# Two chained cross-attentions: x and weights also passed in transposed, row-bias sums on VectorE, the orders of the steps anew

## The reference

```python
# layer 0: softmax over the QUERY axis, residual, layernorm
q = x @ Wq0 + bq0;  k = ctx @ Wk0 + bk0;  v = ctx @ Wv0 + bv0
w = softmax(q @ k.T / 16, axis=queries)
x = layernorm(w @ v + x) * gamma + beta
# layer 1: softmax over the context axis, residual
Q = x @ Wq1 + bq1;  K = ctx @ Wk1 + bk1;  V = ctx @ Wv1 + bv1
out = x + softmax(Q @ K.T / 16, axis=ctx) @ V @ Wo1 + bo1
```

## Time and profile before

| | us |
|---|---|
| timed runs, median of 3 | 467.65 (466.14 to 468.08) |
| profiled execution, first to last instruction (span) | 464.6 |
| TensorE busy | 443.7 (96%) |
| ScalarE busy | 383.7 (83%) |
| VectorE busy | 366.8 (79%) |
| GpSimd busy | 365.0 (79%) |
| granted TensorE clock | 1.000 |

### The profile page before, as it was taken

The page is one execution under the profiler, slowest core; times in us unless marked ns, Lnnn a source line. Parts: engine busy times, 40 slices in busy tenths (PEclk is TensorE's granted clock), DMA queues, the critical chain, the costliest instruction groups (busy, mean ns, idle before and its releaser), DMA issues.

```text
span 464.6 us, 7967 instructions
## 1 busy us (share of the span) xinstructions
PE 443.7 (96%) x2433; PEld 371.6 (80%) x2433; DVE 366.8 (79%) x898; ACT 383.7 (83%) x819; POOL 365.0 (79%) x321
## 2 busy tenths in 40 slices
PE   8798899999999999999999999999999999799796
PEld 8686667887888888888888878888888878687596
DVE  3798978788886988778787888779877887578774
ACT  4899889987999789987899879987899879872473
POOL 0567699979999799887999789987999699963400
PEclk9999999999999999999999999999999999999999
DMA  9400200021100210020200210001100010000001
GB/s 262 130 24 24 71 24 2 23 72 34 36 23 1 72 47 23 24 55 18 70 23 1 71 49 23 24 18 55 46 1 0 3 46 1 0 0 25 23 1 45
DMA packets 23896, 17.29 MB, mean 37 GB/s; under 512 B 1055, under 2 KB 23854, under 8 KB 23854
## 3 DMA queue, kind: packets, MB, share of 16 engines
q1 hardware_dynamic: 23706, 16.66, 11.8%
q10 hardware_dynamic: 148, 0.13, 0.1%
HBM read 12.59 MB, written 4.19 MB: 36 GB/s over the span
## 4 chain that ended last, share of the span: by engine, by line
PE 79%; ACT 8%; DVE 5%; POOL 4%; issue 4%; DVEq 0%; POOLq 0%; ACTq 0%
PE ps_l L654 11%; PE ps_l L655 10%; PE ps_l L656 9%; PE ps_s L800 9%; PE ps_s L654 8%; PE ps_s L656 8%; PE ps_s L655 8%; ACT p L1048 3%; PE ps_s L774 3%; PE ps_s L841 3%; DVE max L1257 2%; POOL wsum L1376 2%; PE ps_l L687 2%; ACT p L1001 2%; PE ps_s L768 2%
## 5 line engine op out<-in xcount | busy, mean ns | idle before, releaser
L1376 POOL TENSOR_TENSOR wsum<-wsum,p 128x512 f32<-128x512 f32 (+1 forms) x88 | 116.3, 1322 | 13.4 <-ACT p L1007 11.8
L1383 POOL TENSOR_TENSOR p_lo<-p,p_hi 128x512 fp32r<-128x512 f32 (+1 forms) x91 | 117.2, 1295 | 2.6 <-ACT p_hi L1015 2.4
L1001 ACT ACTIVATE p<-s_sb,min 128x512 f32<-128x512 f32 (+1 forms) x104 | 75.4, 726 | 7.5 <-DVE min L1171 5.3
L1171 DVE CUSTOM_DVE_ANT_0 s_sb<-ps_l,cb 128x512 f32<-128x512 f32 (+1 forms) x104 | 70.4, 685 | 13.3 <-ACT p L1001 5.5
L1007 ACT ACTIVATE p<-p,r 128x512 f32<-128x512 f32 (+1 forms) x104 | 74.9, 728 | 1.4 <-DVE r L1178 1.3
L1192 DVE TENSOR_TENSOR p1T_lo<-ps_s,p1T_hi 128x512 fp32r<-128x512 f32 (+1 forms) x91 | 60.6, 683 | 14.4 <-ACT p1T_hi L1056 13.9
L1257 DVE TENSOR_REDUCE max<-ps_s 128x1 f32<-128x804 f32 x58 | 57.1, 992 | 10.0 <-PE ps_s L656 8.6
L1056 ACT CAST p1T_hi<-ps_s 128x512 fp32r<-128x512 f32 (+1 forms) x91 | 52.0, 586 | 14.9 <-PE ps_s L800 12.1
L1015 ACT CAST p_hi<-p 128x512 fp32r<-128x512 f32 (+1 forms) x104 | 63.5, 624 | 0.5 <-PE ps_l L656 0.4
L1048 ACT ACTIVATE p<-ps_s,bias 128x1206 f32<-128x1206 f32 (+1 forms) x58 | 53.6, 927 | 3.6 <-DVE bias L1268 3.1
L800 PE MATMUL ps_s<-ident,p 128*128 128x128 f32 (+1 forms) x364 | 49.6, 273 | 1.5 <-ACT p L1048 1.5
(11 more groups left out here) (181 smaller groups left out, 1100.1 us busy)
## 6 DMA issues: line engine op xcount, KB each, us to landing
ctx_sb<-in_ctx_dram SPq DMA_DIRECT2D x24, 256.0 KB, 2.9
x_sb<-in_x_dram SPq DMA_DIRECT2D x8, 512.0 KB, 3.6
out_dram<-y_res SPq DMA_DIRECT2D x16, 256.0 KB, 2.2
p<-in_L_xattn_Wq_dram SPq DMA_DIRECT2D x2, 256.0 KB, 4.2
ctx_sb<-in_ctx_dram SPq DMA_DIRECT2D x8, 32.5 KB
...
```

The source lines that it names most:

```text
L1001: nc.scalar.activation(p0[0:m, ring0(i), :], s0_sb[0:m, (a + i) % 2, :], ACT.Exp, bias=min0[0:m, i:i + 1], scale=-1.0, accum_out=sum0[0:m, ...
L1171: nc.vector.tensor_tensor_reduce(out=s0_sb[0:m, (a + i) % 2, :], in0=ps_s0[0:m, (a + i) % 2, :], in1=cb[a % 2][0:m, :], scale=-SCALE, scal ...
L1376: nc.gpsimd.tensor_tensor(total, total, p0[0:m, ring0(i), :], ALU.add).then_inc(wsum_done, 1)
L1383: nc.gpsimd.tensor_tensor(p0_lo[0:m, h, :], p0[0:m, ring0(i), :], p0_hi[0:m, h, :].bitcast(F32), ALU.subtract).then_inc(p0_lo_done, 1)
```

## The change

The program gets six more inputs, transposed before the launch: x as [8, 256, 512], the two Wq, the two Wk and the second layer's Wv; the seven bias and scale vectors that are needed as columns come as one [128, 2, 7] array. x itself is still passed in.

- turn_x, x_turned, xT_low are gone; `load_xT` loads a batch's transposed x, and project_q0 takes two float32 matmuls.
- turn_wq, turn_wk, turn_vectors and turn_w1 are gone with their copies and the repeated columns; make_w0 and make_w1 work on the loaded transposes.
- weigh_u0 and sum_z0 become `row_bias0`, weigh_u1, bias_row1 and row_bias1 become a new `bias_row1`: for each, four multiply-and-sum instructions of 128 x 256 on VectorE, both inputs in SBUF.
- sum_rows0 transposes wsum by four transposes, and VectorE sums 512 columns in PSUM.
- All four orders are written anew, and the steady part begins at another place (a batch letter d, two ahead, is added). ctx_high waits for the scores of the batch that last used its buffer.

```diff
-                for c in range(EC):
-                    mm = split3(ps_misc[:], a0_hi[:, c, :], a0_lo[:, c, :], xT_hi[:, c, :], xT_lo[:, c, :],
-                                start=(c == 0), stop=(c == EC - 1))
+                for c in range(EC):
+                    mm = nc.tensor.matmul(ps_misc[:], a0_sb[:, c, :], xT_sb[a % 2][:, c, :], start=(c == 0), stop=(c == EC - 1))
...
-                    mm = nc.tensor.matmul(ps_misc[:, t:t + 1], wsum[a % 2][:, t * P:(t + 1) * P], ones[:, 0:1],
-                                          start=True, stop=True)
+                    mm = nc.tensor.transpose(ps_misc[:, t * P:(t + 1) * P], wsum[a % 2][:, t * P:(t + 1) * P], ident[:])
...
+            def load_xT(c):
+                if c >= 2:
+                    sp.wait_ge(qw0_ps, c - 1)
+                sp.dma_start(xT_sb[c % 2][:], xT[bass.ds(c, 1)].rearrange("o (c p) t -> p (o c) t", p=P)
+                             ).then_inc(xT_loaded[c % 2], 16)
...
             def pre0():
-                sp.dma_start(wq_sb[0], wq0.rearrange("(c p) h -> p c h", p=P)).then_inc(w_loaded[0], 16)
+                sp.dma_start(wqT[0], wqT0.rearrange("(h p) e -> p h e", p=P)).then_inc(w_loaded[0], 16)
+                load_xT(0)
                 load_x(0)
...
             for c in range(2, B + 3):
                 if c < B:
+                    load_xT(c)
                     for g in range(GROUPS):
                         load_ctx(c, g)
                     load_x(c)
...
+            def row_bias0(a, _):
+                if a == 0:
+                    dve.wait_ge(u0_done, 1)
+                if a >= 2:
+                    dve.wait_ge(c1_done, TB * (a - 1))
                 if a > 0:
                     dve.wait_ge(cb_ps, a)
+                dve.wait_ge(x_loaded[a % 2], 16 * (a // 2 + 1))
+                for t in range(TB):
+                    nc.vector.tensor_tensor_reduce(out=xr[:, t, :], in0=x_sb[a % 2][:, t, :], in1=u0_row[:], scale=1.0, scalar=0.0,
+                                                   op0=ALU.mult, op1=ALU.add, accum_out=z0[:, t:t + 1]).then_inc(z0_done, 1)
...
             def bias_row1(b, _):
-                dve.wait_ge(u1_part_done, b + 1)
-                nc.vector.tensor_reduce(c1_part[:], xr[:], AX_X, ALU.add).then_inc(c1_part_done, 1)
+                dve.wait_ge(xhat_done, TB * (b + 1))
+                if b == 0:
+                    dve.wait_ge(row1_made, MADE)
+                else:
+                    dve.wait_ge(bias1_done, TB * b)
+                for t in range(TB):
+                    nc.vector.tensor_tensor_reduce(out=xr[:, t, :], in0=xhat[:, t, :], in1=u1_gamma[:], scale=1.0,
+                                                   scalar=c1_const[:, 0:1], op0=ALU.mult, op1=ALU.add,
+                                                   accum_out=c1[:, t:t + 1]).then_inc(c1_done, 1)
...
             def bias_x0(a, _):
-                nc.vector.tensor_copy(rowsum0[:], ps_misc[:, 0:TB]).then_inc(rowsum_done, 1)
+                nc.vector.tensor_reduce(rowsum0[:], ps_misc[:].rearrange("p (t m) -> p t m", m=P), AX_X, ALU.add
+                                        ).then_inc(rowsum_done, 1)
```

More of the change, by code:

```diff
@@ new lines @@
+    ("p0_low", 1, 1), ("rsqrt_var", 0, 0), ("rsqrt_var", 0, 1), ("sum_weights", 1, 2), ("p0_low", 1, 2),
+    ("p0_low", 1, 3), ("sum_weights", 1, 3), ("ctx_low", 1, 1), ("sum_weights", 1, 4), ("sum_weights", 1, 5),
+    ("p0_low", 1, 4), ("p0_low", 1, 5), ("ctx_low", 1, 2), ("sum_weights", 1, 6), ("p0_low", 1, 6),
+    ("sum_weights", 1, 7), ("p0_low", 1, 7), ("p0_low", 1, 8), ("residual1", 0, 0), ("p0_low", 1, 9),
+    ("sum_weights", 1, 8), ("sum_weights", 1, 9), ("sum_weights", 1, 10), ("sum_weights", 1, 11),
@@ L309 @@
-    ("sum_weights", 6, 8), ("ctx_low", 6, 3), ("p0_low", 6, 9), ("sum_weights", 6, 9), ("p0_low", 6, 10),
-    ("residual1", 5, 0), ("p0_low", 6, 11), ("sum_weights", 6, 10), ("sum_weights", 6, 11), ("sum_weights", 6, 12),
-    ("p0_low", 6, 12), ("sum_weights", 7, 1), ("p0_low", 7, 0), ("ctx_low", 7, 0), ("rsqrt_var", 6, 0),
-    ("p0_low", 7, 1), ("p0_low", 7, 2), ("rsqrt_var", 6, 1), ("weigh_u1", 6, 0), ("ctx_low", 7, 1),
-    ("sum_weights", 7, 2), ("ctx_low", 7, 2), ("sum_weights", 7, 3), ("p0_low", 7, 3), ("p0_low", 7, 4),
@@ L314 @@
-    ("sum_weights", 7, 4), ("ctx_low", 7, 3), ("sum_weights", 7, 5), ("p0_low", 7, 5), ("p0_low", 7, 6),
-    ("sum_weights", 7, 6), ("sum_weights", 7, 7), ("sum_weights", 7, 8), ("p0_low", 7, 7), ("sum_weights", 7, 9),
-    ("p0_low", 7, 8), ("p0_low", 7, 9), ("sum_weights", 7, 10), ("p0_low", 7, 10), ("residual1", 6, 0),
-    ("sum_weights", 7, 11), ("p0_low", 7, 11), ("sum_weights", 7, 12), ("p0_low", 7, 12), ("rsqrt_var", 7, 0),
-    ("rsqrt_var", 7, 1), ("weigh_u1", 7, 0), ("residual1", 7, 0),
+    ("sum_weights", 6, 10), ("sum_weights", 6, 11), ("sum_weights", 6, 12), ("p0_low", 6, 11), ("p0_low", 6, 12),
@@ new lines @@
+    ("residual1", 5, 0), ("ctx_low", 7, 0), ("sum_weights", 7, 1), ("p0_low", 7, 0), ("rsqrt_var", 6, 0),
+    ("rsqrt_var", 6, 1), ("p0_low", 7, 1), ("p0_low", 7, 2), ("sum_weights", 7, 2), ("sum_weights", 7, 3),
+    ("p0_low", 7, 3), ("ctx_low", 7, 1), ("ctx_low", 7, 2), ("p0_low", 7, 4), ("sum_weights", 7, 4), ("p0_low", 7, 5),
+    ("sum_weights", 7, 5), ("sum_weights", 7, 6), ("p0_low", 7, 6), ("p0_low", 7, 7), ("sum_weights", 7, 7),
+    ("sum_weights", 7, 8), ("sum_weights", 7, 9), ("ctx_low", 7, 3), ("p0_low", 7, 8), ("p0_low", 7, 9),
@@ L319 @@
+    ("p0_low", 7, 10), ("sum_weights", 7, 10), ("sum_weights", 7, 11), ("sum_weights", 7, 12), ("p0_low", 7, 11),
+    ("p0_low", 7, 12), ("residual1", 6, 0), ("rsqrt_var", 7, 0), ("rsqrt_var", 7, 1), ("residual1", 7, 0),
 )
@@ L871, in make_a, with row_of @@
                 return mm
+            def row_of(ps, col, rows_in):
+                for h in range(EC):
+                    mm = nc.tensor.matmul(ps, col[:, h:h + 1].broadcast_to([P, P]), rows_in[:, h, :],
+                                          start=(h == 0), stop=(h == EC - 1))
+                return mm
             def keep_warm(n):
@@ L1114, in _ @@
+                act.dma_start(cols[:], columns).then_inc(cols_loaded, 16)
             steps = {f.__name__: f for f in (
-                x_turned, q0_high, bias0, ctx_high, ctx_split, exp0, norm0, p0_high, weighed0, y_turned, row_bias1, q1_high, exp1,
-                p1_turned, weighed1, p1_turned_half, weighed1_half, copy_w1)}
+                q0_high, bias0, ctx_high, ctx_split, exp0, norm0, p0_high, weighed0, y_turned, q1_high, exp1,
+                p1_turned, weighed1, p1_turned_half, weighed1_half, copy_w0, copy_w1)}
@@ L1350, in _ @@
             steps = {f.__name__: f for f in (
-                ctxT_low, xT_low, at0_low, bias_x0, q0_low, weigh_u0_first, sum_z0, max0, recip0, residual0, moments0, normalised, bias_row1,
+                ctxT_low, at0_low, bias_x0, q0_low, row_bias0, max0, recip0, residual0, moments0, normalised, bias_row1,
                 q1_low, rowmax1, bias1_of, recip1, p0_low_first, p1_low, p1_low_half, finish, prepare_w1)}
@@ L1429, in _ @@
             steps = {f.__name__: f for f in (
-                ctx_low, sum_weights, p0_low, rsqrt_var, weigh_u0, weigh_u1, residual1)}
+                ctx_low, sum_weights, p0_low, rsqrt_var, residual1)}
             pre0()
@@ L1447 @@
     for name in _INS:
-        a = np.ascontiguousarray(inputs[name])
+        if name == "columns":
+            a = np.stack([inputs[n] for n in COLUMNS]).reshape(len(COLUMNS), -1, P).transpose(2, 1, 0)
+        elif name in TURNED:
+            a = np.swapaxes(inputs[TURNED[name]], -1, -2)
+        else:
+            a = inputs[name]
+        a = np.ascontiguousarray(a)
         arrays[f"in_{name}_dram"] = a
```

360 lines of the change are left out of this document (112 added, 248 removed), and 467 rows, old and new, of tables (GPSIMD_HEAD, GPSIMD_STEADY, SCALAR_HEAD, SCALAR_STEADY).

## The result

The changed kernel takes 499.45 us (median of 4 runs, 498.41 to 500.01) against 467.38 (466.14 to 468.08): ratio 1.0691, 95% interval 1.0668 to 1.0713. I had forecast 458.5, range 451 to 474, with 0.19 on slower. The forecast is wrong by 41 us and in its sign.

The account below looks back on a forecast made before the run. TensorE was taken to bound the kernel, nearly always busy in the middle. Gains 6.7 + 1.9 + 1.0 + 2.0, less 2.5 for waiting passes, made 9.1 us: span 455.5, time 458.5 us, range 451 to 474.

Parts of the forecast that it names:

- TensorE, each batch: Net TensorE work removed, 0.91 us a batch; over seven batches plus batch 0's sums, a 6.7 us gain.
- The totals' 0.35: In sum_rows0, four transposes (0.44 us) replace column sums of wsum (0.79), 0.35 us less TensorE work.
- The two float32 matmuls, 1.72: In project_q0, the added pair of 512 columns takes 1.72 us, as the same pair does in project_q1.
- The start: Before batch 0's first max: it comes at 13.4 us instead of 15.35, a 1.9 us gain, bounds 0 and 3.
- the 1.0 for the second layer's weights: Dropping turn_w1's transposes on TensorE and two ScalarE copies gains 1.0 us, bounds 0.5 to 2.
- What the passes wait for: VectorE's eight new row-bias passes wait for GpSimd 0.1 us each: 0.35 a batch, 2.5 us lost in all.
- The 38.28 pass: A 0.793 us VectorE multiply-and-sum, read as starting its own time when a GpSimd pass ended at 38.78.
- rival 1: Row-bias group ahead of q1_low alternates with GpSimd's 6.4 us queue, 1.29 us a turn: 484.5 us, chance 0.2.
- The cover of 0.2 us: Slack ahead of q1_low: max0 ends at 4.5 us after normalised, TensorE wants its score buffer at 4.7.
- Other edits: Loads, ctx_high's new wait and residual1 priced at 0; bias_x0 meeting residual1's passes at 0 to 0.7 us each.
- GpSimd's relief (2.0): GpSimd losing two products gains 2.0 us of TensorE's idle time at the ends, bounds 0 and 6.
- the new order (at most 0.24 a batch): New order of steps: the middle holds 0.24 us of idle a batch to be won, no more.

Follow-up runs that it names:

- kernel 5: Kernel before the change with only the float32 projection from a loaded transposed x, without turn_x, x_turned, xT_low: 464.36 us, ratio 0.9941.
- kernel 11: Changed kernel with one-input row-bias sums, GpSimd waiting for normalised, and residual1 of batches 1 to 5 waiting for bias_x0: 468.98 us, ratio 1.0049.
- kernel 7: Kernel 6 with one wait more: GpSimd's first operation of the next batch waits for the end of bias_x0; 464.82 us, ratio 0.9958.
- kernel 6: Kernel 5 with the totals of the weights taken by four transposes and a 512-element VectorE reduction: 483.67 us, ratio 1.0359.
- kernel 1: Changed kernel with both row-bias groups as plain one-input sums, multiply by u and constant left out: 486.43 us, ratio 1.0411.
- kernel 12: Kernel before the change with only the row biases moved to VectorE's multiply-and-sum passes, in its old order: 518.19 us, ratio 1.1114.
- kernel 2: Changed kernel in its new orders with the row-bias products back on GpSimd and sums on VectorE: 504.32 us, ratio 1.0772.

## Why the prediction was wrong, by its steps

**TensorE, each batch (0.91).** Right in size where little waits: kernel 5 shows its 0.56, and kernel 11's periods hold 52.3 us of TensorE's work instead of 53.1. The changed kernel's page shows nothing of the 8 us that TensorE was to be less busy: 447.0 us against 443.7, and 52.88 a batch against 53.10. The clock at half adds up to 8.5, and a matmul's record behind a wait is longer (0.50 us at 239.12, 0.39 behind it); I did not break it down further. The totals' 0.35 did not show (0.04 in kernel 7); the step itself went from 0.81 to 0.36 us from its start to the next one's (202.90 in kernel 5, 208.66 in kernel 6), and what fills the difference I did not trace.

**The two float32 matmuls, 1.72.** Held with the clock full: the pair spans 1.88 us in the timeline, as project_q1's did before. In batch 1, in the stretch at half clock, it spans 3.26.

**The start (1.9).** First max at 14.03, so 1.3 us earlier than before and 0.6 later than said. Yet batch 0's normalised came at 60.03 against 56.77: 3.3 us lost. The rows of the start that show it, TensorE's, then VectorE's (in brackets idle time and cause):

```profile
25.76 0.50 PE L629 MATMUL ps_l<-p_hi,ctx_lo 128*128 128x512 f32 x1 [3.29 <-DVE p_lo L1076]
```

```profile
22.55 1.48 DVE L1203 TENSOR_TENSOR p<-p 128x256 f32<-128x256 f32 x1 [1.11 <-DMA p<-in_L_xattn_bo_dram]
23.95 1.75 DVE L1076 TENSOR_TENSOR p_lo<-p,p_hi 128x512 fp32r<-128x512 f32 x1
```

VectorE waits 1.11 us for a load, and then two passes meet GpSimd, which runs two sums of weights from 22.48 to 25.15. Behind the wait comes the first stretch at half clock, and the second lies around 60.03 itself.

I followed the start only up to the first max and took it for granted that what comes behind keeps its lead. Its 1.9 and the 3.3 make 5.2 of the 41 us, and the 1.0 for the second layer's weights is in no run by itself.

**What the passes wait for (2.5).** This is the step that failed. I had both ends, 0 and 1.29 us a pass, and chose 0.1 by 13 passes of p_lo that stand singly in batch 0, beside a half-full GpSimd. A single pass waits at most for the rest of one GpSimd pass; a group waits for one whole pass at each of its members, and the row for a group (0.42 from start to start) was taken where GpSimd stood still. The 38.28 pass was read too well: it ended 0.29 us behind the GpSimd pass (39.07 and 38.78), where a free one takes 0.48, so "to the hundredth" is wrong, though it did wait. And 0.1 for each of eight passes less 0.2 of cover makes 0.6 us a batch, not 0.35. The mechanism was rival 1, told with its 6.4 us queue. What was measured: 13.0 us for the two row-bias groups in this order (kernel 1), 51 in before's (kernel 12). The cover of 0.2 us that I worked out ahead of q1_low was near: bias_row1 ended 4.9 us after normalised instead of 3.3, and TensorE lost 1.22 of the difference of 1.6 there.

**Other edits.** "bias_x0 may now meet residual1's 0.74 us passes: 0 to 0.7 each" was in the text and not in the sum. Its passes took 0.96 instead of 0.48, three in a group. And as a group that would wait, normalised was not in the text at all. Both together are the greater part: from kernel 1 to kernel 11, 17.5 us, the clock's share in it included. I had asked which new instructions meet GpSimd; the question was which of all VectorE's groups meet it in the new order. With the totals I named the 0.69 us reduction as VectorE work (it is 0.67) and put it nowhere in time, although the four passes stand right behind it and GpSimd's next pass began 1.40 us after their start. Kernel 6 shows the price of that shift: 19 us.

**TensorE's clock.** The prediction had it at full speed throughout and no term for it. In the changed kernel it costs up to 8.5 us, and it goes with the long waits: what makes TensorE wait is paid a second time in part.

**GpSimd's relief (2.0), the new order (at most 0.24 a batch).** The bound on the order was one-sided: an order can win no more than the idle time, but it can lose whatever it moves together. GpSimd's relief is in no run by itself; in kernel 11 the stretch from the last normalised to the end is 41.3 us, before 40.1. And its products had also been a guard. weigh_u1 waited for xhat (0.85 us in the earlier trace rows) and weigh_u0 for VectorE's z (11.0 us in all in the earlier trace rows), so GpSimd stood still there. Kernel 2 shows the guard: with weigh_u1 back behind rsqrt_var, normalised fell from 0.850 to 0.409.

**What is left.** In the changed kernel the seven periods took 396.7 us (60.03 to 456.71), 29.0 more than before; with 3.3 at the start and 1.2 at the end that is all of its longer span. Kernel 11 is 10.5 us above 458.5. By its marks of normalised (60.03 to 425.94) its seven periods took 365.9 us, before 367.7 (56.77 to 424.49): 1.8 gained where 6.4 was said, with TensorE still idle 0.9 us a batch, most of it waiting for xhat. The start lost 3.3 and the end 1.2. bias_x0 still meets GpSimd in batches 0, 1 and 7 (its mean is 0.573).

**Rivals.** Rival 1 forecast 484.5 for one group of four, the one ahead of q1_low; its mechanism was right. That its number came within 15 us is partly luck. For its own group it was too dear: 26 us, where both row-bias groups together cost 13.0. The queue was as long as it said (230.28 to 236.75), but normalised and finish used up its first 4 us. In exchange normalised and bias_x0, which it did not name, cost more than that. TensorE's wait for the minimum once a batch, which it named as a sign, came (3.6 us in 3). Its test ("mean near 1.3") was between the two, 0.861 by the mean over waiting and free passes (median 0.484, longest 1.503): a mean over passes that either wait or don't says little, and GpSimd running dry ends the waiting early.
